# A layered FFT-convolution kernel: DVE alone builds the row matrices, ACT copies their high parts and spreads six of the sixteen groups, and the last rows of the first image load between the stores

## The reference, cut to what matters

```python
x = x + conv_in_frequency_domain(groupnorm(x), w_real, w_imag, b_real, b_imag)   # rfftn, 3x3 complex conv, irfftn
x = x + mean_filter_15x15(groupnorm(x))                                         # x: (8, 16, 512, 512) f32
```

## Time and profile before

| | us |
|---|---|
| median of 3 runs | 4029.41 (4027.86 to 4030.45) |
| the profiled execution | 4030.95 |
| its span | 4028.9 |
| last group spread (start 183.38, 3.34 long) | 186.72 |
| start of the sixteen rows' load (setup_done) | 95.5 |

### The profile page before, as it was taken

One profiled execution on the slowest core, in us unless ns is written; L12 is line 12 of the kernel. 1 busy time (PEld: TensorE's weight loads), 2 busy tenths in 40 slices (PEclk: granted clock), 3 DMA queues, 4 the chain that ended last, 5 costly groups with the idle time before them and its releaser, 6 DMA issues.

```text
span 4028.9 us, 122552 instructions
## 1 busy us (share of the span) xinstructions
PE 3515.2 (87%) x42592; PEld 2538.7 (63%) x42592; DVE 3445.0 (86%) x6382; ACT 2382.8 (59%) x3774; POOL 2638.3 (65%) x2177
## 2 busy tenths in 40 slices
PE   3199889998999989899798998999898998999988
PEld 1166576665766667666675666666576665766667
DVE  7889977998779978899788997789977998789976
ACT  0078733886248852588427883288733886248852
POOL 5088853887538865588546885388853986538865
PEclk8599999999999999999999999999999999999999
DMA  6511166111741128311382114711165111741114
GB/s 161 169 43 53 44 173 178 52 53 34 225 135 52 52 57 245 91 51 52 100 239 57 51 53 141 208 45 53 42 184 167 52 52 38 222 134 51 52 53 137
DMA packets 228530, 407.91 MB, mean 101 GB/s; under 512 B 98160, under 2 KB 173520, under 8 KB 215888
## 3 DMA queue, kind: packets, MB, share of 16 engines
q1 hardware_dynamic: 205776, 285.88, 24.6%
q10 hardware_dynamic: 22400, 117.46, 10.9%
HBM read 256.31 MB, written 146.80 MB: 100 GB/s over the span
## 4 chain that ended last, share of the span: by engine, by line
PE 52%; DVE 21%; issue 11%; POOL 8%; ACT 5%; ACTq 1%; DVEq 1%; SPq 1%; DMA 0%; POOLq 0%
PE h_ps L658 14%; PE p L549 11%; PE h_ps L453 9%; PE p L684 6%; PE p L491 4%; POOL ob_all L1306 3%; DVE arena L1104 3%; DVE ob_all L1152 3%; DVE half_row L1171 3%; PE xt_ps L443 3%; DVE img L1161 2%; POOL ob_all L1308 2%; POOL arena L1299 2%; DVE ob_all L1231 2%; ACT arena L727 1%
## 5 line engine op out<-in xcount | busy, mean ns | idle before, releaser
L549 PE MATMUL p<-arena,bd_all 64*64 64x512 f16 x16896 | 1206.4, 379 | 30.0 <-DVE ob_all L1152 29.6
L1299 POOL TENSOR_TENSOR arena<-arena 128x512 f16<-128x512 f32 x512 | 594.1, 1160 | 495.7 <-ACT arena L760 476.2
L453 PE MATMUL h_ps<-hilbert,arena 128*128 128x256 f16 x6144 | 754.5, 272 | 115.8 <-DVE arena L1104 111.9
L549 PEld LDWEIGHTS p<-arena,bd_all 64*64 64x64 f16 x16896 | 604.4, 106 | 385.6 <-issue 38.8
L453 PEld LDWEIGHTS h_ps<-hilbert,arena 128*128 128x128 f16 x6144 | 564.0, 97 | 398.7 <-issue 317.9
L1357 POOL TENSOR_TENSOR arena<-img 128x512 f32<-128x512 f32 x392 | 499.0, 1274 | 469.4 <-PE h_ps L658 443.9
L727 ACT ACTIVATE arena<-h_ps 128x512 f16<-128x512 f32 x512 | 305.7, 597 | 841.4 <-PE h_ps L658 593.9
L1308 POOL TENSOR_TENSOR ob_all<-ob_all,img 128x512 f32<-128x512 f32 x512 | 662.7, 1294 | 75.6 <-POOL ob_all L1306 60.6
L1306 POOL TENSOR_TENSOR ob_all<-ob_all 128x512 f32<-128x512 f32 x512 | 655.8, 1281 | 52.5 <-DVE ob_all L1152 51.9
L766 ACT ACTIVATE arena<-xt_ps 128x1024 f16<-128x1024 f16 x512 | 520.7, 1017 | 35.5 <-PE xt_ps L443 35.5
L658 PE MATMUL h_ps<-bd_all,arena 128*128 128x128 f32 x3584 | 539.5, 286 | 0.0
(11 more groups left out here) (163 smaller groups left out, 4980.6 us busy)
## 6 DMA issues: line engine op xcount, KB each, us to landing
out<-ob_all SPq DMA_DIRECT2D x512, 256.0 KB, 4.2
bd_all<-bd_dram SPq DMA_DIRECT2D x512, 192.0 KB, 2.3
img<-in_x ACTq DMA_DIRECT2D x168, 512.0 KB, 7.3
img<-in_x ACTq DMA_DIRECT2D x112, 256.0 KB, 4.8
wrap_mat<-tab_wrap_h SPq DMA_DIRECT2D x512, 32.0 KB, 2.0
img<-in_x SPq DMA_DIRECT2D x24, 512.0 KB, 23.1
bd_dram<-ob_all SPq DMA_DIRECT2D x16, 768.0 KB, 3.5
img<-in_x SPq DMA_DIRECT2D x16, 256.0 KB, 7.2
```

Of the source, the lines that this page charges most:

```text
L453: m = mm(dst(a), xT[:, 4 * lx + k, 0:rows], tb["hilbert16"][:, lt, k, 0:cols], start=(half == 0 and i == 0), stop=(half == 1 and i == 2))
L549: m = mm(bank[out_half * HP:(out_half + 1) * HP, :], bd[s % RB][rows, 6 * lm + (j if own else j + 1), :], part, start=opens and i3 == 0, s ...
L1299: G.tensor_tensor(gp[s][:, 1, :], g32, gp[s][:, 0, :], ALU.subtract).then_inc(g_split, 1)
```

## The change

Three things change, all in the setup. First, DVE makes all six terms of `smat`; for each it only makes `full` (four operations) and the low part, and ACT casts `full` to the high part. The low part of term j-1 is made after term j, from four scratch buffers in place of two. POOL has only its `sum_weights`. Second, ACT spreads groups 1, 3, 5, 7, 9 and 11, each with four activations of 128x768 elements scaled by a column of `edge`; DVE spreads the other ten, does none of the row counts ahead of `setup_done` and counts up to seven rows after each of its groups. Third, SP issues the load of two rows (a pair, two DMAs) ahead of each of the first eight stores, instead of all sixteen rows ahead of them all.

```diff
-        base_ready, pool_matrices = sem("base_ready"), sem("pool_matrices")
+        full_made, full_high, bd_made_act = sem("full_made"), sem("full_high"), sem("bd_made_act")
...
         scratch = [flat[:, 2048 + i * T * C:2048 + (i + 1) * T * C].rearrange("p (t o) -> p t o", o=C)
-                   for i in range(2)]
-        scratch_g = [flat[:, 4096 + i * T * C:4096 + (i + 1) * T * C].rearrange("p (t o) -> p t o", o=C)
-                     for i in range(2)]
+                   for i in range(4)]
...
+        def by_scalar_engine(g):
+            return g % 2 == 1 and g < 12
+
+        def groups_made(g):
+
+            return sum(by_scalar_engine(k) == by_scalar_engine(g) for k in range(g + 1))
+
+        def stage_rows(g):
+            return (stage[g % 2][:, 0:GROUP_T * REC].rearrange("p (q c h) -> p q c h", c=C, h=HL),
+                    smat[:, g * GROUP_T:(g + 1) * GROUP_T].rearrange("p t j o -> p (t j) o"))
...
             sp.wait_ge(setup_done, 1)
-            for t in range(T - LAG, T, 2):
-                load_pair(0, t)
             for g in range(T // GROUP_T):
-                sp.wait_ge(bd_made, g + 1)
+                if g < LAG // 2:
+                    load_pair(0, T - LAG + 2 * g)
+                sp.wait_ge(bd_made_act if by_scalar_engine(g) else bd_made, groups_made(g))
...
+            for j in range(6):
+                act.wait_ge(full_made, j + 1)
+                copy(smat[:, :, j], scratch[2 * (j % 2) + 1]).then_inc(full_high, 1)
             act.wait_ge(setup_done, 1)
+            for g in range(T // GROUP_T):
+                if by_scalar_engine(g):
+                    if g >= 2:
+                        act.wait_ge(bd_stored[g % 2], 16 * (g // 2))
+                    staged, terms = stage_rows(g)
+                    for h in range(HL):
+                        ins = nc.scalar.activation(staged[:, :, :, h], terms, ACT.Identity, scale=edge[:, h:h + 1])
+                    ins.then_inc(bd_made_act, 1)
...
-            act.wait_ge(bd_made, T // GROUP_T)
+            act.wait_ge(bd_made, groups_made(T // GROUP_T - 1))
+            act.wait_ge(bd_made_act, groups_made(11))
...
-            dve.sem_inc(base_ready, 1)
-            row_matrices(V, link, scratch, range(0, 4))
+
+            def low_matrices(j):
+
+                dve.wait_ge(full_high, j + 1)
+                link(V.tensor_tensor(smat[:, :, 6 + j], scratch[2 * (j % 2) + 1], smat[:, :, j], ALU.subtract))
...
+                scr, full = scratch[2 * (j % 2):2 * (j % 2) + 2]
+                link(V.tensor_tensor(scr, part(1), trig(0), ALU.mult))
+                link(V.tensor_tensor(full, scr, part(0), ALU.add))
+                link(V.tensor_tensor(scr, part(2), trig(1), ALU.mult))
+                V.tensor_tensor(full, scr, full, ALU.add).then_inc(full_made, 1)
+                if j >= 1:
+                    low_matrices(j - 1)
+            low_matrices(5)
...
-            for t in range(T // 4):
-                count_row(0, t)
-            dve.wait_ge(pool_matrices, 6 * 2)
+            link(V.tensor_copy(edge[:, 0:HL], tb["hl_mask16"][:]))
             V.memset(sc[:, 16:17], 0.0).then_inc(setup_done, 1)
 
-            rest = iter(range(T // 4, T))
+            rest = iter(range(T))
             for g in range(T // GROUP_T):
+                if by_scalar_engine(g):
+                    continue
...
-                for t in itertools.islice(rest, 3):
+                for t in itertools.islice(rest, 7):
                     count_row(0, t)
...
-            row_matrices(G, link, scratch_g, range(4, 6))
-            pool.wait_ge(setup_done, 1)
...
-            for k in range(made[0], NCH):
+            for k in range(NCH):
                 sum_weights(0, k)
+            pool.wait_ge(setup_done, 1)
```

More of the change, by code:

```diff
@@ L947, in _, with part, trig @@
             combine(lambda j: base[:, :, j], ar, ai, 1, 1)
-            dve.sem_inc(base_ready, 1)
-            row_matrices(V, link, scratch, range(0, 4))
+            def low_matrices(j):
+                dve.wait_ge(full_high, j + 1)
+                link(V.tensor_tensor(smat[:, :, 6 + j], scratch[2 * (j % 2) + 1], smat[:, :, j], ALU.subtract))
+            for j in range(6):
+                def part(f):
+                    return base[:, f, j].unsqueeze(1).broadcast_to([P, T, C])
+                def trig(f):
+                    return tb["trig_swapped" if j % 2 else "trig_h"][:, f].unsqueeze(2).broadcast_to([P, T, C])
+                scr, full = scratch[2 * (j % 2):2 * (j % 2) + 2]
[6 more added lines that the diff above has]
+            low_matrices(5)
             for blk, krow, col, swap, sr, si in ((0, 0, 1, False, 1, 1), (0, 0, 2, True, 1, -1),
@@ L973, in count_row @@
                 V.bn_stats(stat[:, t, :], img[:, t, :]).then_inc(rows_counted, 1)
-            for t in range(T // 4):
-                count_row(0, t)
-            dve.wait_ge(pool_matrices, 6 * 2)
+            link(V.tensor_copy(edge[:, 0:HL], tb["hl_mask16"][:]))
             V.memset(sc[:, 16:17], 0.0).then_inc(setup_done, 1)
-            rest = iter(range(T // 4, T))
+            rest = iter(range(T))
             for g in range(T // GROUP_T):
+                if by_scalar_engine(g):
+                    continue
                 if g >= 2:
                     dve.wait_ge(bd_stored[g % 2], 16 * (g // 2))
[L983 to L986, removed]
+                staged, terms = stage_rows(g)
+                V.tensor_tensor(staged, terms.unsqueeze(3).broadcast_to([P, 12 * GROUP_T, C, HL]),
                                 tb["hl_mask16"][:].unsqueeze(1).unsqueeze(1).broadcast_to([P, 12 * GROUP_T, C, HL]),
                                 ALU.mult).then_inc(bd_made, 1)
-                for t in itertools.islice(rest, 3):
+                for t in itertools.islice(rest, 7):
                     count_row(0, t)
```

## The result

| | before | changed |
|---|---|---|
| median, us | 4028.64 (4 runs, 4022.97 to 4030.45) | 4002.70 (4 runs, 3999.43 to 4006.24) |
| profiled execution / its span | 4030.95 / 4028.9 | 4006.24 / 4004.1 |
| setup_done | 95.36 | 75.99 |
| end of the last spread group | 186.72 | 161.29 |

The ratio is 0.9938, with a 95% interval of 0.9921 to 0.9955: 25 us faster by the ratio and 26 by the medians, where I forecast 37. Set on the median that I started from, it gives 0.9938 x 4029.41 = 4004.4, just past the upper end of my range. The span shrank by 24.8 us and the end of the spreading came 25.4 earlier, so the reading of what counts held: what DVE's path loses in the setup, the span loses, and nothing was given back later. What fell short is in the setup.

What follows compares the result with a forecast made beforehand. DVE's setup path alone was taken to bound image 0: setup_done at 76.3 plus 73.1 of spreading ends at 149.4 instead of 186.72, 37.3 us earlier, so the median 4029.41 becomes 3992.1 us; range 3986 to 4003.

Steps and rivals of the forecast that it cites:

- row matrices: DVE's six terms of five operations at the setup's start: 41.4 us instead of 48.3, a gain of 6.9.
- tiny operations: DVE's 24 short operations after the row matrices: 5.5 us instead of 8.3, a gain of 2.8.
- What bounds the kernel: Image 0 waits for DVE's setup path alone, until the last spread group ends at 186.72 us.
- The spreading before: Spreading in the old kernel: 16 groups, 48 counted rows and a 12.22 us store wait made 91.4 us.
- The loads between the stores: Spreading on the mixed DMA queue: the 12.22 us first-store wait goes, DVE waits 2.5 us in all.
- ACT's groups: Six spread groups on ACT, four activations each at 0.89 us, so 3.6 us a group.
- the text's own formula: Spreading time through slot 1: six times ACT's group plus 3.8 us for store and handover, then 18.2 from group 13.
- the second rival: ACT's spread costs 1.6 us an activation: spreading takes 79.4 us, 6.3 more, time 3998.4; chance 0.06.
- the third: ACT three times as slow as DVE, 9.8 us a group: spreading 99.8 us, 26.7 more, time 4018.8; chance 0.04.
- The threshold: DVE needs slot 1 for group 13 at 54.9 us after setup_done, which holds for ACT groups under 5.35 us.
- rival 4: Slower than before: ACT's groups hold slot 1 and, by SP's store order, DVE's even groups; 4039.2 at 3.3 an activation; chance 0.03.
- The rule of the ScalarE page: Against spreading on ACT: gives multiplies and relu to VectorE, called up to about 3x faster per element in 16 bits.

Runs made afterwards that it cites:

- the first experiment: The changed kernel with ACT's four activations of a group writing four blocks with step 1 (output laid out wrongly); 3989.17 us, ratio 0.9906 to the kernel before.

## Why the prediction was wrong, step by step

| Step | forecast | measured |
|---|---|---|
| row matrices | 41.4 | 40.7 |
| tiny operations | 5.5 | 5.3 |
| setup_done | 76.3 | 75.99 |
| an activation of ACT's spread | 0.89 | 1.78 |
| DVE's waits for stores | 2.5 | 14.5 |
| setup_done to the end of spreading | 73.1 | 85.3 |
| gain | 37.3 | 25.4 at the end of spreading, 25 by the ratio |

- *What bounds the kernel.* Right. In the ten profiles of this document, the span less the end of the last spread lies between 3836.6 and 3842.8, while the end itself moves from 139 to 187.
- *Row matrices and tiny operations.* Right within 0.7 us, with the turns that DVE and POOL take priced from one meeting of the two.
- *The spreading before.* The 91.4 us hold 45 counted rows ahead of the last group's end and not the 48 that I wrote (52.5 + 27.0 + 12.2 = 91.7). Nothing in the sum of the forecast rests on it.
- *The loads between the stores.* Right: with fast activations the spreading took 73.8 us in the first experiment, against 73.1, with 3.2 of waits. In the changed kernel it is worth 11.4 us.
- *ACT's groups.* This is the step that failed, the sentence "I take 0.89, since its two rows have the same scale operand, and read steps have cost little": an activation took 1.78. Both rows were for writes with step 1. The one row that wrote with a step, 531 ns for 256 elements of f32 with step 2, stood for the bound of 1.6. I read it as a far end, though it was the only one of the rows with a write step, and its write spans 512 positions where the changed activation's spans 3072. With 7.12 in the text's own formula, 6 x (7.12 + 3.8) + 18.2 = 83.7 of the 85.3 measured: the mechanism and its place (slot 1, group 13) were in the text, but at this size only between the second rival (6.4 us a group) and the third (9.8), with chances of 0.06 and 0.04. Most of the remaining 1.6 us are round trips, idle time included, of 4.05 on average in place of 3.8.
- *The threshold.* That ACT is free below 5.35 us a group was worked out for group 13 alone. It left out that ACT's stores hold up DVE's in SP's order: 13.4 of the 14.5 us of waits are in slot 0, ahead of groups where the sum had 2.5. The text had this only as rival 4, with a chance of 0.03. Four groups on ACT ended no earlier than six. Whether ACT would be free just below 5.35 no run tests; at 3.41 the waits are 3.2.
- *The rule of the ScalarE page* (the Trainium skill, ScalarE: Activation LUTs, Rules for kernel authors) I set aside as hardly borne out. The page gives its factor of up to 3 for single-source operations in bf16; DVE's spread reads two tensors in f16. The advice came out right here, a group costing ACT 7.12 and DVE 3.28, 2.2 times, but DVE's rate isn't the reason: with step 1 ACT's group is 3.41 to DVE's 3.28, so it was ACT's write that was slow.

## What to carry to other kernels

Price a moved operation by a row that writes in the same pattern, not by one that has the same operands and length; where no such row exists, put the operation into idle time and measure it before building on it. When a helper engine works through one buffer, its pace is its own time plus the store's round trip, and that sum is to be compared with the time of the engine that it helps. Where stores of two engines stand in one order, the slower engine also holds up the other's stores. A further buffer can be worth more than a faster operation: here 19 us by the medians (4002.70 to 3983.66) with two more groups on ACT, against 13.5 (to 3989.17) for activations at half their time with the old split.

## What the hardware showed that I had not expected

- ACT's writes to SBUF pay for the positions that they span: 0.93 us for 768 f16 with step 1, 1.15 with step 2, 1.59 with step 3, 1.99 with step 4, and 1.99 for 384 elements with step 8. The Trainium skill (SBUF — State Buffer, the note on cachelines in Door 1: The DMA port swizzle) says that eight bf16 elements can be strided for free. For ACT's writes of f16, of the same width, the run differs: step 2 already costs 1.15 for 0.93.
- Loads issued between stores mostly hold SP longer: in the changed kernel the first pair, ahead of all stores, took 1.21 us to issue and the seven pairs behind stores 1.84 to 2.30, while sixteen loads in a row took 10.48 in the kernel before, 1.31 a pair. What decides it wasn't shown; one pair behind a store, in the kernel with four groups on ACT, took 1.19.

```profile
76.24 1.21 SPq L337 DMA_DIRECT2D img<-in_x  x2
79.34 0.42 SPq L360 DMA_DIRECT2D bd_dram<-ob_all  x1
79.81 1.93 SPq L337 DMA_DIRECT2D img<-in_x  x2
```
